# Layer 2 of a four-layer GNN kernel: DMA transposes the f16 parts of the probabilities, and DMA stacks each head's query and key parts over 128 rows

## The reference

```
h = max(layernorm(x), 0)
q, k, v = h @ Wq.T + bq, h @ Wk.T + bk, h @ Wv.T + bv      # 8 heads of 32
scores = (q_h @ k_h.T) / sqrt(32), -inf where adj == 0
attn = softmax(scores);  out_h = attn @ v_h
x = x + concat(out) @ Wo.T + bo
```

## Time and profile before

| | |
|---|---|
| median of 3 runs | 2096.86 us (2090.93 to 2097.89) |
| profiled execution | 2089.51 us, span 2087.9 us |
| mean granted TensorE clock | 0.976 of full speed |
| busy: PE, PEld, DVE, ACT, POOL | 91%, 85%, 87%, 69%, 29% |
| DMA | 43.85 MB, the queue on SP 6.1% of 16 engines |

### The profile page before, as it was taken

One profiled execution on the slowest core, in us unless ns is written; L12 is line 12 of the kernel. 1 busy time (PEld: TensorE's weight loads), 2 busy tenths in 40 slices (PEclk: granted clock), 3 DMA queues, 4 the chain that ended last, 5 costly groups with the idle time before them and its releaser, 6 DMA issues. The chain is left out here.

```text
span 2087.9 us, 45990 instructions
## 1 busy us (share of the span) xinstructions
PE 1905.1 (91%) x15944; PEld 1781.3 (85%) x15944; DVE 1822.3 (87%) x6095; ACT 1448.2 (69%) x3378; POOL 609.8 (29%) x756
## 2 busy tenths in 40 slices
PE   1899999999999999999999999999999999999985
PEld 1789888988888989888898888889888899898874
DVE  6688999989999988989998898999889899998774
ACT  2467677777677777767777776777776677876664
POOL 4122332222332332233233233323223322322222
PEclk8899999999999999999999999999999999999997
DMA  5000000000000000000000000000000000000000
GB/s 153 11 17 11 22 22 11 22 11 22 22 22 11 22 17 17 21 22 19 14 22 17 17 22 22 12 21 22 15 18 21 21 12 22 17 12 16 17 16 11
DMA packets 31206, 43.85 MB, mean 21 GB/s; under 512 B 3328, under 2 KB 26880, under 8 KB 30976
## 3 DMA queue, kind: packets, MB, share of 16 engines
q1 hardware_dynamic: 30976, 40.91, 6.1%
HBM read 32.38 MB, written 8.52 MB: 20 GB/s over the span
## 5 line engine op out<-in xcount | busy, mean ns | idle before, releaser
L707 POOL TENSOR_SCALAR ea<-ea,rs 128x256 f32<-128x256 f32 x256 | 140.0, 559 | 476.8 <-DVE rs L1316 476.8
L691 POOL TENSOR_TENSOR rstd<-ve,pow_half 128x2 f32<-128x2 f32 x160 | 119.4, 746 | 488.3 <-DVE ve L1197 486.2
L1093 PE MATMUL ps<-kp,qp 32*128 32x256 f32 x1536 | 250.1, 295 | 3.8 <-DVE kp L1345 3.4
L852 ACT ACTIVATE pb<-lg,hmin 128x256 f32<-128x256 f32 x512 | 231.6, 505 | 19.0 <-DVE hmin L1366 18.4
L899 PE MATMUL ps<-wout,hid 128*128 128x256 f32 x1536 | 230.2, 290 | 4.2 <-ACT hid L866 4.2
L1093 PEld LDWEIGHTS ps<-kp,qp 32*128 32x128 f32 x1536 | 197.7, 185 | 41.5 <-issue 22.9
L1366 DVE CUSTOM_DVE_ANT_0 lg<-ps,maskp 128x256 f32<-128x256 f32 x512 | 195.0, 417 | 33.8 <-PE ps L1093 31.2
L899 PE MATMUL ps<-pT,whs 128*128 128x256 f32 x1536 | 213.4, 288 | 11.0 <-DVE pT L1325 9.7
L899 PEld LDWEIGHTS ps<-pT,whs 128*128 128x128 f32 x1536 | 191.7, 191 | 20.5 <-DVE pT L1325 16.2
L899 PEld LDWEIGHTS ps<-wout,hid 128*128 128x128 f32 x1536 | 197.1, 190 | 6.4 <-ACT hid L866 5.6
L729 POOL TENSOR_TENSOR hid<-fu,hid 128x512 fp32r<-128x512 f32 x96 | 127.0, 1322 | 255.9 <-ACT hid L866 255.9
(11 more groups left out here) (180 smaller groups left out, 4739.6 us busy)
## 6 DMA issues: line engine op xcount, KB each, us to landing
tbc<-t_dram SPq DMA_DIRECT2D x32, 512.0 KB, 3.6
xin<-x_in SPq DMA_DIRECT2D x32, 256.0 KB, 2.7
out<-xs SPq DMA_DIRECT2D x32, 256.0 KB, 2.2
t_dram<-tb SPq DMA_DIRECT2D x128, 1.0 KB
xs<-a_heads SPq DMA_DIRECT2D x4, 128.0 KB, 5.9
pT<-a_heads SPq DMA_DIRECT2D x4, 128.0 KB, 4.6
lg<-W_out SPq DMA_DIRECT2D x2, 256.0 KB, 5.6
tb<-adj SPq DMA_DIRECT2D x1, 256.0 KB, 2.7
```

The costliest lines, as they stand in the source:

```text
L707: last = pool.tensor_scalar(ea(g)[:, c, :], ea(g)[:, c, :], rs[g][:, c:c + 1], 1.0, ALU.mult, ALU.mult)
L852: last = act.activation(pb[h % 2][:, c, :], lg[h % 2][:, c, :], ACT.Exp, bias=hmin[h % 2][:, c:c + 1], scale=-1.0)
L1093: last = pe.matmul(bank(BA)[:, c, :], qp[r, a, oc, blk(c)], kp[r, b, oc, :], start=(n == 0), stop=(n == 2))
```

## The change

The two parts of q and k are no longer used where they lie. After `q_lo` and `k_lo`, SP copies them by DMA inside SBUF: for group p of 32 rows (heads p and p+4) four copies of 32 rows each put the parts under one another, the query as high, high, low, low and the key as high, low, high, low (`q_stack`, `k_stack`; 32 copies a batch of 32 x 512 f32). One matmul over all 128 rows then makes one half of a head's scores: two matmuls a head in place of six. The fourth product, low by low, comes in as well. Heads alternate between banks BA and BB.

The probabilities are split before they are transposed: `s_exp` writes back into `lg`, now three buffers; `p16_hi` on ACT makes the high f16 part; `p16_lo` on POOL makes the low part, in place of DVE. Then one DMA transpose on SP (`p_T`) moves both parts, 128 x 1024 f16, into `pT16`. It waits for `p16_lo(h)` and for `values(h-2)`. Three buffers of `p16` are in turn. The planner gets new costs and hand-over times, and its priorities (`LEAD`) stay. A smaller scratch area for generated DMA descriptors makes room.

```
-    XB, XI, PT = 4, 2, 2
+    XB, XI, PT, LG, LP = 4, 2, 2, 3, 3
...
-        HOP = ((0.0, 0.2, 0.2, 0.2, 5.0), (0.22, 0.15, 0.15, 0.17, 0.2), (0.25, 0.13, 0.13, 0.16, 5.0),
-               (0.16, 0.07, 0.06, 0.1, 5.0), (3.5, 3.5, 3.5, 3.5, 0.0))
+        HOP = ((0.0, 0.2, 0.2, 0.2, 0.2), (0.22, 0.15, 0.15, 0.17, 0.2), (0.25, 0.13, 0.13, 0.16, 0.2),
+               (0.16, 0.07, 0.06, 0.1, 0.2), (2.5, 2.5, 2.5, 2.5, 0.0))
...
-                a("scores", h, TE, 0.7, ("q_lo", 0), ("k_lo", 0), ("smin", h - 1))
...
+                a("q_stack", p, SY, 1.2, ("q_lo", 0))
...
+                a("p16_lo", h, PO, 1.2, ("p16_hi", h))
+                a("p_T", h, SY, 2.0, ("p16_lo", h), ("values", h - 2))
...
+                def stack(p, u, parts, stacked, of_row):
+                    for j in range(4):
+                        sp.dma_start(f(stacked)[DH * j:DH * j + DH, p],
+                                     f(parts)[DH * p:DH * p + DH, of_row[j]]).then_inc(heads_stacked[p], 16)
+
+                def stack_q(p, u):
+                    sp.wait_ge(q_lo, u + 1)
+                    stack(p, u, qp, qs, (0, 0, 1, 1))
...
+                def transpose_probs(h, u):
+                    sp.wait_ge(p16_lo, of(u, h, HQ))
+                    if h >= 2:
+                        sp.wait_ge(o_done, of(u, h - 2, HQ))
+                    sp.dma_start(pT16[h % 2][:].rearrange("p t c n -> p (t c n)").rearrange("p (m n) -> p m n", n=P),
+                                 p16[of(u, h, HQ) % LP][:].rearrange("p t c n -> p (t c n)"), transpose=True)\
+                        .then_inc(p_turned[of(u, h, HQ) % LP], 16)
...
+                def low_of_probs(h, u):
+                    pool.wait_ge(p16_hi, of(u, h, HQ))
+                    pool.tensor_tensor(p16[of(u, h, HQ) % LP][:, 1], lg[h % LG][:], p16[of(u, h, HQ) % LP][:, 0], ALU.subtract).then_inc(p16_lo, 1)
...
                 def softmax_exp(h, u):
                     act.wait_ge(min_ready, of(u, h, HQ))
-                    if h >= 2:
-                        act.wait_ge(p_turned, of(u, h - 2, HQ))
...
+                        last = act.activation(lg[h % LG][:, c, :], lg[h % LG][:, c, :], ACT.Exp,
+                                              bias=hmin[h % LG][:, c:c + 1], scale=-1.0)
...
+                def high_of_probs(h, u):
+                    act.wait_ge(p_done, of(u, h, HQ))
...
                 def scores(h, u):
...
-                    r, oc = slice(DH * (h % 4), DH * (h % 4) + DH), h // 4
+                    pe.wait_ge(heads_stacked[h // 2], 128 * (u + 1))
+                    if h >= 2:
+                        pe.wait_ge(min_ready, of(u, h - 2, HQ))
...
-                            last = pe.matmul(bank(BA)[:, c, :], qp[r, a, oc, blk(c)], kp[r, b, oc, :],
-                                             start=(n == 0), stop=(n == 2))
+                        last = pe.matmul(bank(scores_bank(h))[:, c, :], qs[:, h // 2, h % 2, blk(c)],
+                                         ks[:, h // 2, h % 2, :], start=True, stop=True)
...
-                def low_of_turned(h, u):
-                    dve.wait_ge(pT16_hi, of(u, h, HQ))
-                    dve.tensor_tensor(pT16[h % 2][:, 1], bank(BB), pT16[h % 2][:, 0], ALU.subtract)\
-                        .then_inc(pT16_lo, 1)
...
-    nc = bacc.Bacc("TRN2", target_bir_lowering=False, num_devices=1)
+    nc = bacc.Bacc("TRN2", target_bir_lowering=False, num_devices=1, dynamic_dma_scratch_size=1024)
```

More of the change, by code:

```diff
@@ L89, in adj_preln_kernel @@
         kp = sb("kp", [P, 2, C, N], F32R)
+        qs = sb("qs", [P, 4, 2, N], F32R)
+        ks = sb("ks", [P, 4, 2, N], F32R)
         v3 = sb("v3", [P, C, HQ, VC], BF16)
-        lg = [sb(f"lg{k}", [P, C, N]) for k in range(2)]
-        pb = [sb(f"pb{k}", [P, C, N]) for k in range(2)]
+        lg = [sb(f"lg{k}", [P, C, N]) for k in range(LG)]
+        p16 = [sb(f"p16{k}", [P, 2, C, N], F16) for k in range(LP)]
         pT16 = [sb(f"pT16{k}", [P, 2, C, N], F16) for k in range(2)]
@@ L121, in adj_preln_kernel @@
         dmin, zz, npeak, psums, rs = (columns_of(n, HG + 2) for n in ("dmin", "zz", "npeak", "psums", "rs"))
-        hmin = [sb(f"hmin{k}", [P, C]) for k in range(2)]
+        hmin = [sb(f"hmin{k}", [P, C]) for k in range(LG)]
         rden = sb("rden", [P, 2 * C])
@@ L643, in adj_preln_kernel @@
         v_a, v_r, v_b, v_c = (sem(n) for n in ("v_a", "v_r", "v_b", "v_c"))
[L644 to L645 removed]
+        s_done, min_ready, p_done = (sem(n) for n in ("s_done", "min_ready", "p_done"))
+        p16_hi, p16_lo, o_done, o_used = (sem(n) for n in ("p16_hi", "p16_lo", "o_done", "o_used"))
+        heads_stacked = each("heads_stacked", HQ // 2)
+        p_turned = each("p_turned", LP)
         wo_done = sem("wo_done")
@@ L677, in spread, with stack_k @@
                     sp.dma_start(tbc[:], t_dram[u % 2:u % 2 + 1].broadcast_to([P, HG, N])).then_inc(t_spread, 16)
-                program = dict(load=load, store=store, t_spread=spread)
+                def stack(p, u, parts, stacked, of_row):
[5 more added lines that the diff above has]
+                    stack(p, u, qp, qs, (0, 0, 1, 1))
+                def stack_k(p, u):
+                    sp.wait_ge(k_lo, u + 1)
+                    stack(p, u, kp, ks, (0, 1, 0, 1))
+                def transpose_probs(h, u):
[5 more added lines that the diff above has]
+                        .then_inc(p_turned[of(u, h, HQ) % LP], 16)
+                program = dict(load=load, store=store, t_spread=spread, p_T=transpose_probs,
+                               q_stack=stack_q, k_stack=stack_k)
                 for name, k, u in order:
@@ L1111, in values @@
                         for n, (part, kc) in enumerate(((0, 0), (0, 1), (1, 0), (1, 1))):
-                            last = pe.matmul(ps[:, at0:at0 + VC], pT16[h % 2][:, part, kc, blk(c)],
-                                             v3[:, kc, h, :], start=(n == 0), stop=(n == 2 * C - 1))
+                            last = pe.matmul(ps[:, at0:at0 + VC], pT16[h % 2][:, part, c, blk(kc)],
+                                             v3[:, kc, h // 2 + h % 2 * (HQ // 2), :], start=(n == 0), stop=(n == 2 * C - 1))
                     last.then_inc(o_done, 1)
@@ L1433, in _ @@
                                q_lo=low_of_q, k_lo=low_of_k, v_r=value_rest, smin=score_minimum,
-                               pT16_lo=low_of_turned, gather=gather_values, normal=normalise, x3=x_plus_context,
+                               gather=gather_values, normal=normalise, x3=x_plus_context,
                                f1_lo=low_of_ffn, y=ffn_sum, y_gamma=times_gamma, final=result)
```

63 lines of the change are left out of this document (26 added, 37 removed).

## The result

The changed kernel takes 2284.51 us (median of 4 runs, 2279.3 to 2292.4), where 2093.89 us stand beside it for the kernel before (4 runs): a ratio of 1.091, 95% interval 1.087 to 1.096. It is 191 us slower. The forecast was 1940.

What follows compares the result with a forecast made beforehand. PE bounds the kernel at 58.6 us a batch, DVE close at 55.7; afterwards DVE, 51.6, ends last. Period 61.5 falls to 55.6: 2089.5 - 166 + 9 = 1932.5, plus 7 gives 1940 us; range 1860 to 2200.

Steps and rivals of the forecast that it cites:

- The failed step: DMA queue on SP: 32 stacking copies of 64 KB a batch, 0.35 us each, 11.2 us, bounds 9.0 to 15.0.
- the queue's sum: SP's issue time a batch: 3.1 us existing, 11.2 copies, 16 transposes, together 30 of 56 us, so not the limit.
- The new wait: First batch's layer 2, standing alone: copies, a landing and one transpose's path add about 9 us, once.
- The DVE step: DVE waiting behind POOL's instructions: stall grows from 2.1 to 3.4 us a batch, +1.3, bounds -2.1 to +2.6.
- the sign that the prediction named: On DVE, the row scaling's mean rises over 540 ns with its median at 405, showing the lock with POOL.
- The transposes: DMA queue: 8 transposes of 256 KB a batch, 2.0 us issue each and 2.2 to land, 16 us a batch.
- Rival (c): Transposes hold the DMA queue over 5.2 us each; at 6.5 us, 66.3 us a batch, 2255 us; chance 0.24.
- The buffer's turn: Transpose waits for value matmul two heads earlier: 5.2 us per two heads, 21 us for eight, well inside 56.
- The fill: DVE's busy share of the period: between its 0.906 and PE's 0.952, giving 57.0 to 54.2, middle 55.6 us.

## Why the prediction was wrong

**The failed step.** "Added: 32 stacking copies of 64 KB ... I take 0.35 (the spread's), 11.2 us." One copy takes 0.63 us in a row of them, above the upper bound of 0.47; 32 take 20.2 us a batch, above the bound of 15.0. That the queue's sum still came out near, 33 us against 30, is luck: the copies were 9.0 too low, the transposes 6.1 too high. The bounds came from copies over 128 partitions and from rows of 1 KB; no row had the shape, 32 partitions of 2 KB.

The larger fault is where the term was put. The copies were added to the queue's sum, found to fit into the period, and priced at nothing for all but the first batch. They are not free, although the queue is half empty: removing them alone, in an unchanged order, saves 216 us, or 7.0 us for each of the 31 later batches. Copies stand between `k_lo` and the first score, and ahead of layer 3's row stores in the queue. The prediction did say that the spread has little slack, but put only waiting transposes ahead of it, not copies. The new wait was named for the first batch only, at 9 us; the first store in fact comes 31 us later (255.62 against 224.30).

**The order.** The order printed ahead of the prediction shows eight query copies in front of the first key copy, and the prediction did not ask what that does to the first score. With 2.5 for four copies in place of 1.2 the planner alternates them, and 93 us go. Since an order can shift the time by itself, that figure isn't purely the alternation's.

**Right, near and missed.** PE works 53.7 us a batch against 48.3: of the excess, 16 x 0.116 = 1.9 us lie in the score matmuls, and where the rest lies was not resolved; the granted clock was 0.90 where the costs had been read at 0.99. DVE: 52.2 against 51.6. POOL's subtraction: 1173 ns against 1143; 28.1 us a batch against 27.6. The high part on ACT: 622 ns against 629.

**The DVE step.** Moving the low part to POOL left DVE's other work 2.0 us a batch longer in one pair of runs, where I took 1.3 within -2.1 to 2.6. That single DVE instructions wait for POOL's is shown in the trace of the kernel before: of the 228 row scalings of 128x256 (L1210) that start between 200 and 2000 us, 176 took at most 416 ns, among them all 147 with no POOL instruction beside them, and the other 52 took 500 ns or more and ended 145 to 155 ns after the end of a POOL instruction. The slow one of the pair in the earlier trace rows took 740 ns. How much such waiting would grow was an estimate, and the 2.0 us are not where I read it. Scaling in the changed kernel:

```profile
L1235 DVE TENSOR_SCALAR tb<-xs,mv,rstd 128x256 f32<-128x256 f32 x128 | 56.1, 481 | 6.9 <-POOL rstd L723 6.5
...
L1235 DVE TENSOR_SCALAR tb<-xin,mv,rstd 128x256 f32<-128x256 f32 x64 | 34.9, 587 | 1.9 <-POOL rstd L723 1.9
```

The first form fell from a mean of 540 ns while POOL grew busier, and the second rose from 518; the sign that the prediction named, a mean over 540, failed. Where the 2.0 us lie was not resolved. In the pair with three buffers DVE works 51.7 and 55.9 us a batch and its subtractions take 8 x 0.811 = 6.5, which leaves 2.3; in the pair with four it works 52.8 and 58.5, the subtractions take 8 x 0.792 = 6.3, and 0.7 is left. Since the order alone moves DVE's work by 1.3 us a batch with the same instructions, these runs bound the 1.3 us of growth but don't show that the 2.0 are contention.

**The transposes.** Issue 1.24 us and landing 3.1, against 2.0 and 2.2: the unknown price was overestimated in the queue. The prediction ended with what a slower kernel would mean, a transpose that was mis-sized in the queue; it was mis-sized the other way, and the slower kernel came from the copies. Rival (c) gave 2255 us and so comes nearest in time, but its mechanism is false: it needed more than 5.2 us of queue for each. The buffer's turn, reckoned at 21 of 56 us, was indeed no limit: with a looser wait (three buffers, same order) the time stays at 2122.6. The 0.5 us for semaphores in it was an allowance that no row showed; in the changed kernel 0.05 us pass from a transpose's landing to the value matmul that waited for it (median of 26).

**The remainder.** Without copies 2053 us were measured, not 1940. The forecast had DVE at 51.6 us of work and 93% fill, 55.6 us a batch; measured are 53.6 us and 89.6%, 59.8. By these numbers about half of the gap between 55.6 and 59.8 is work, half fill, an estimate. The fill was taken between those of two engines in the kernel before, whose order had been made for other work. The runs show that an order alone is worth 91 us; whether one exists that brings the stacked form near 1940 stays open.

## What to carry to other kernels

A DMA that feeds the next step is charged to that step's chain first, then to the chain of whatever stands behind it in the queue, and only then to the queue's sum; a half-empty queue says nothing about its price (here 7.0 us a batch for 32 copies, with the queue taken up for 33 of 66 us). Where a planner writes the order, any edit of a dependency, price or buffer count makes a new order, and here that alone moved the time by up to 91 us: before a gain or loss is put down to an edit, run the edit in the old order, or the new order without the edit. Look for the price of a small copy in rows of its own shape, partitions and row length, not of its bytes.

## What the runs showed of the hardware

- A copy inside SBUF of 32 partitions by 2 KB issues in 0.59 us (0.63 with the gap to the next), where 256 KB over 128 partitions issue in 0.40: fewer bytes, longer issue.
- A DMA transpose of 128 x 1024 f16 issues in 1.24 us and lands after 3.1 (medians of 256).
- Small stores behind a few large transfers were waited for longer: from the issue of four row stores of 1 KB to the spread that waits for them 6.9 us pass behind eight loads of 256 KB, 2.0 us in the changed kernel.
- In the middle of the run the granted clock was 0.90 with the copies, with PE busy 82% of the time, 0.95 without them in the same order (88%), and 0.99 before (95%). The busy share alone doesn't settle it: with the copies added to the kernel before it was 0.95 at 82%, and with the repriced transposes 0.93 at 91%. A score matmul comes to 0.266 us with the copies and 0.211 (108.2/512) in the run without copies and their plan.
